# A decoder layer with a mixture of experts: expert results added up in DRAM by accumulating scatters

## The reference, cut to what matters

```
x = x + attention(layernorm(x))            # 16 heads of 64, causal, gated
x = x + retention(layernorm(x), ctx, ctx)  # 16 heads of 8, decay mask
x = x + ffn(layernorm(x))
```

```
topw, sel = top_k(x @ Wg, 3);  topw = softmax(topw)
y_e = gelu(x @ Wup[e] + bup[e]) @ Wdown[e] + bdown[e]     # 128 -> 512 -> 128
ffn(x) = sum over the 3 chosen experts of topw * y_e
```

## Time and profile before

| what | value |
|---|---|
| median of 3 runs | 521.89 us (521.81 to 523.43) |
| profiled execution: time | 523.74 us |
| profiled execution: span of the core | 522.0 us |
| granted TensorE clock, mean | 0.965 |
| PE busy | 457.5 us (88% of the span) |
| DVE busy | 393.2 us (75%) |
| ACT busy | 329.3 us (63%) |
| POOL busy | 256.1 us (49%) |
| DMA read and written in DRAM | 18.91 MB, 11.44 MB |

### The profile page before, as it was taken

The page is one execution under the profiler, slowest core; times in us unless marked ns, Lnnn a source line. Parts: engine busy times, 40 slices in busy tenths (PEclk is TensorE's granted clock), DMA queues, the critical chain, the costliest instruction groups (busy, mean ns, idle before and its releaser), DMA issues.

```text
span 522.0 us, 12401 instructions
## 1 busy us (share of the span) xinstructions
PE 457.5 (88%) x3540; PEld 374.1 (72%) x3540; DVE 393.2 (75%) x1359; ACT 329.3 (63%) x1001; POOL 256.1 (49%) x398
## 2 busy tenths in 40 slices
PE   1689998999999999999999999976697798999980
PEld 1467786877777678687777767854466688999980
DVE  4755477988888888798888888889688766665556
ACT  3558865875776686687577668643445565776660
POOL 3400005157355535726735653575175764666861
PEclk9989999999999999999999999998798898999995
DMA  8990000000000000000000000001045242222248
GB/s 268 367 225 1 1 0 3 1 16 15 10 7 18 15 0 22 13 5 15 15 10 9 19 12 0 22 17 48 20 143 156 68 107 56 74 71 62 63 112 214
DMA packets 40803, 30.06 MB, mean 58 GB/s; under 512 B 3795, under 2 KB 36999, under 8 KB 40768
## 3 DMA queue, kind: packets, MB, share of 16 engines
q1 hardware_dynamic: 36864, 22.63, 15.5%
q0 software_dynamic: 3472, 6.49, 4.0%
q10 hardware_dynamic: 432, 0.53, 0.4%
HBM read 18.91 MB, written 11.44 MB: 58 GB/s over the span
## 4 chain that ended last, share of the span: by engine, by line
PE 52%; DVE 18%; ACT 8%; issue 8%; SPq 5%; POOL 5%; DMA 3%; DVEq 0%; ACTq 0%; POOLq 0%
PE zb L801 8%; PE sc L840 6%; PE ob L869 6%; PE xb L918 4%; PE zb L1074 3%; PE ob L1074 3%; PE xb L943 3%; PE sc L801 2%; PE tb_a L801 2%; ACT pT L667 2%; PE tb_a L853 2%; PE tb_b L853 2%; PE sc L834 2%; DVE nmx L1187 2%; ACT p_sb L660 2%
## 5 line engine op out<-in xcount | busy, mean ns | idle before, releaser
L651 ACT ACTIVATE qk<-zb 128x512 f32<-128x512 f32 x64 | 38.2, 597 | 66.9 <-PE zb L801 66.9
L520 POOL TENSOR_TENSOR spare_p<-tri 128x1 f32<-128x1 f32 x71 | 14.8, 209 | 125.3 <-DVE xn L1268 67.4
L600 POOL DMA_INDIRECT results_by_token<-y_sb,row_i x59 | 60.3, 1022 | 22.3 <-issue 21.8
L658 ACT ACTIVATE p_sb<-sc,nmx 128x128 f32<-128x128 f32 x128 | 47.1, 368 | 33.9 <-DVE nmx L1187 33.5
L660 ACT ACTIVATE p_sb<-sc,nmx 128x256 f32<-128x256 f32 x128 | 61.0, 476 | 0.0
L840 PE MATMUL sc<-qk 64*128 64x256 f32 (+1 forms) x512 | 60.4, 356 | 0.2 <-ACT qk L651 0.2
L869 PE MATMUL ob<-pT,v_sb 128*64 128x256 f32 (+1 forms) x512 | 58.2, 350 | 1.3 <-DVE oT L1205 1.3
L840 PEld LDWEIGHTS sc<-qk 64*128 64x128 f32 x512 | 45.1, 190 | 15.6 <-issue 10.1
L533 POOL DMA_INDIRECT tokens_by_expert<-packed,slot_i x48 | 48.2, 1005 | 8.6 <-issue 7.4
L1205 DVE TENSOR_TENSOR oT<-ob,pT 128x256 f32<-128x256 f32 x64 | 26.9, 420 | 27.1 <-PE ob L869 27.1
L869 PEld LDWEIGHTS ob<-pT,v_sb 128*64 128x64 f32 x512 | 32.3, 141 | 20.8 <-issue 11.2
(11 more groups left out here) (294 smaller groups left out, 1375.4 us busy)
## 6 DMA issues: line engine op xcount, KB each, us to landing
xg<-tokens_by_expert SPq DMA_DIRECT2D x24, 130.0 KB, 2.2
tokens_by_expert<-padding SPq DMA_DIRECT2D x12, 260.0 KB
wup_all<-in_L_ffn_Wup SPq DMA_DIRECT2D x1, 3072.0 KB, 14.4
wdn_all<-in_L_ffn_Wdown SPq DMA_DIRECT2D x12, 256.0 KB, 5.7
wkv_sb<-in_L_attn_Wkv SPq DMA_DIRECT2D x2, 512.0 KB, 6.5
ctx_b<-in_ctx SPq DMA_DIRECT2D x8, 128.0 KB, 2.1
out<-x_all SPq DMA_DIRECT2D x4, 256.0 KB, 3.3
results_by_token<-y_sb,row_i POOLq DMA_INDIRECT x59
```

The lines of the kernel that those rows point to most:

```text
L600: pool.indirect_dma_start(out=ys, out_offset=bass.IndirectOffsetOnAxis(ap=row_i[:, u, a:a + 1], axis=0), in_=y_sb[:, u, a, :], in_offset=None,
L658: act.activation(p_sb[:, w, h, 0:P], sc[:, k, S:S + P], ACT.Exp, bias=nmx[:, w, 0, n:n + 1], accum_out=total[:, w, 0, h:h + 1])
```

## The change

The results are no longer written to rows of their own and added on VectorE, but added up in DRAM. There are two arrays, `sums_of_even_tiles` and `sums_of_odd_tiles`, each with a row for every token and 512 more rows for padding. The scatter of tile n goes to array n % 2 with `compute_op=ALU.add`: the DMA reads the old row, adds, and writes the sum. As two such DMAs on the same rows must not overlap, each waits until the last scatter to its array (tile n-2) has landed. The even array starts as `x2b`: `keep` is now a store by SyncE, and VectorE's next `second_residual` waits for it before it overwrites `x2b`. The odd array is cleared at the start with one DMA from `padding`. Padding rows carry valid row numbers (the 512 rows behind the tokens) in place of `SKIP`, and the bounds check goes. At the end each chunk needs two loads, the even sums straight into `x_all`, and one addition.

```diff
--- before.py
+++ after.py
@@ -39,7 +39,6 @@
 PAD = S + SLOTS
 ROWS = E * CAP + SLOTS
 ROW = D + 2
-SKIP = 1 << 20
 FOUT = 4
 SCALE = DH ** -0.5
 NEG = -3.0e38
@@ -217,7 +216,7 @@
             wv_hi, wv_lo = early("wv_hi", [P, H * DH]), early("wv_lo", [P, H * DH])
             wqk_hi, wqk_lo = early("wqk_hi", [P, 2, H * DH]), early("wqk_lo", [P, 2, H * DH])
         hT = sb("hT", [P, 2, HC, SLOTS])
-        y_in = sb("y_in", [P, TOPK * FOUT * D])
+        sb("rest_of_state", [P, TOPK * FOUT * D])
         y_sb = sb("y_sb", [P, DEPTH, HALVES, D])
         wup_hi = sb("wup_hi", [P, 2, HID], F32R)
         wup_lo = sb("wup_lo", [P, 2, HID], F32R)
@@ -225,9 +224,7 @@
         xgT_lo = sb("xgT_lo", [P, 2, SLOTS], F32R)
         xg = sb("xg", [P, DEPTH, HALVES, ROW])
         sb("rest_of_early", [P, 512])
-        y3 = [a[:, 0:TOPK * FOUT * D].rearrange("p (k n d) -> p k n d", k=TOPK, n=FOUT) for a in (
-            wkv_sb, y_in,
-            p_sb[:, :, :, :].rearrange("p a h k -> p (a h k)"), pT[:, :, :, :].rearrange("p a h k -> p (a h k)"))]
+        odd_sums = wkv_sb[:, :].rearrange("p (n d) -> p n d", n=NT)
         kv_last = wkv_sb[:, :].rearrange("p (t a n) -> p t a n", t=T, a=2)
         spare = sb("spare", [P, 1])
         spare_p = sb("spare_p", [P, 3 + T * TOPK])
@@ -288,7 +285,7 @@
             sem(n) for n in ("ld_x", "ld_xs", "ld_wq", "ld_wk", "ld_wv", "ld_wo", "ld_n", "ld_g", "ld_tab", "ld_bd", "ld_ctx", "ld_up", "ld_dn", "stored"))
         ld_e = [sem(f"ld_e{u}") for u in range(DEPTH)]
         scattered = [sem(f"scattered{u}") for u in range(DEPTH)]
-        dispatched, padded, ld_y = sem("dispatched"), sem("padded"), [sem(f"ld_y{c}") for c in range(NT // FOUT)]
+        dispatched, padded, cleared, kept, ld_y = sem("dispatched"), sem("padded"), sem("cleared"), sem("kept"), [sem(f"ld_y{c}") for c in range(NT // FOUT)]
         consts = sem("consts")
         consts_v = sem("consts_v")
         tables_ready = sem("tables_ready")
@@ -303,8 +300,8 @@
         a_P, a_PA, a_qk, a_hi_wv, a_PT, a_V, a_xT, a_xN, a_ge, a_xn3T, a_el = (
             sem(n) for n in ("a_P", "a_PA", "a_qk", "a_hi_wv", "a_PT", "a_V", "a_xT", "a_xN", "a_ge", "a_xn3T", "a_el"))
         a_kv, v_kv = sem("a_kv"), sem("v_kv")
-        p_kv, p_q, p_sum, p_ret, p_pack, p_keep, p_cell, p_chain = (
-            sem(n) for n in ("p_kv", "p_q", "p_sum", "p_ret", "p_pack", "p_keep", "p_cell", "p_chain"))
+        p_kv, p_q, p_sum, p_ret, p_pack, p_cell, p_chain = (
+            sem(n) for n in ("p_kv", "p_q", "p_sum", "p_ret", "p_pack", "p_cell", "p_chain"))
         pe_CNT, v_hit, v_filled, v_slot, v_pad, v_first, v_plan, v_fin = (sem(n) for n in ("pe_CNT", "v_hit", "v_filled", "v_slot", "v_pad", "v_first", "v_plan", "v_fin"))
         f_row = sem("f_row")
         f_T, f_hi, f_w, f_xg, f_up, f_gelu, f_dn, f_y, f_out = (
@@ -312,7 +309,7 @@
 
 
         xs = nc.dram_tensor("tokens_by_expert", (ROWS, ROW), F32, kind="Internal").ap()
-        ys = nc.dram_tensor("results_by_token", (TOPK * N, D), F32, kind="Internal").ap()
+        ys = [nc.dram_tensor(f"sums_of_{name}_tiles", (N + PAD, D), F32, kind="Internal").ap() for name in ("even", "odd")]
 
         def at(b, per, k):
 
@@ -364,9 +361,22 @@
                 sp.dma_start(wdn_all[:, e, :, :], f_wdown[e].rearrange("(c p) d -> p c d", p=P)).then_inc(ld_dn, 16)
 
             ctx_v = ctx.rearrange("b (t p) d -> b p t d", p=P)
-            with sp.Fori(0, B - 1) as i:
-                sp.wait_ge(p_kv, at((i, 1), T, 0))
-                sp.dma_start(ctx_b[:, :, :], ctx_v[bass.ds(i + 1, 1)].rearrange("a p t d -> p (a t) d")).then_inc(ld_ctx, 16)
+            kept_v = ys[0][0:N, :].rearrange("(b t p) d -> b p t d", t=T, p=P)
+
+            def keep(b):
+
+                sp.wait_ge(v_x2, at(b, 1, 1))
+                to = kept_v[b] if isinstance(b, int) else kept_v[bass.ds(b[0], 1)].rearrange("a p t d -> p (a t) d")
+                sp.dma_start(to, x2b[:, :, :]).then_inc(kept, 16)
+
+            sp.wait_ge(tables_ready, 8)
+            sp.dma_start(ys[1].rearrange("(n p) d -> p n d", p=P), bc(padding[:, 0, 0:D], 1, (N + PAD) // P)).then_inc(cleared, 16)
+            sp.wait_ge(p_kv, T)
+            sp.dma_start(ctx_b[:, :, :], ctx_v[1]).then_inc(ld_ctx, 16)
+            with sp.Fori(0, B - 2) as i:
+                sp.wait_ge(p_kv, at((i, 2), T, 0))
+                sp.dma_start(ctx_b[:, :, :], ctx_v[bass.ds(i + 2, 1)].rearrange("a p t d -> p (a t) d")).then_inc(ld_ctx, 16)
+                keep((i, 0))
 
 
             def load(n):
@@ -390,12 +400,14 @@
             sp.wait_ge(v_first, 1)
             for n in range(DEPTH):
                 load(n)
+            keep(B - 2)
             sp.wait_ge(v_pad, 1)
             with sp.Fori(0, E) as i:
                 r = sp.value_load(pad_row[0:1, bass.ds(i, 1)], min_val=0, max_val=E * CAP - PAD)
                 sp.dma_start(xs[bass.ds(r, PAD), :].rearrange("(a p) w -> p a w", p=P), padding[:, :, :]).then_inc(padded, 16)
             for n in range(DEPTH, EARLY):
                 load(n)
+            keep(B - 1)
             sp.wait_ge(v_plan, 1)
             for n in range(EARLY, TILES):
                 if n == BIG - 1:
@@ -407,11 +419,10 @@
                                      max_val=results_before(TILES + (u - TILES) % DEPTH)) for u in range(DEPTH)]
             for u in range(DEPTH):
                 sp.wait_ge(scattered[u], reached[u])
-            y_v = ys.rearrange("(k n p) d -> p k n d", k=TOPK, p=P)
             for c in range(NT // FOUT):
-                for k in range(TOPK):
-                    n = slice(c * FOUT, (c + 1) * FOUT)
-                    sp.dma_start(y3[c][:, k, :, :], y_v[:, k, n, :]).then_inc(ld_y[c], 16)
+                n = slice(c * FOUT, (c + 1) * FOUT)
+                for sums, to in zip(ys, (x_all, odd_sums)):
+                    sp.dma_start(to[:, n, :], sums[0:N, :].rearrange("(n p) d -> p n d", p=P)[:, n, :]).then_inc(ld_y[c], 16)
             out_v = out.rearrange("b (t p) d -> p (b t) d", p=P)
             for c in range(NT // FOUT):
                 n = slice(c * FOUT, (c + 1) * FOUT)
@@ -448,10 +459,10 @@
             pool.iota(steps256[:, :], [[SLOTS, N // SLOTS]], base=0, channel_multiplier=0, **exact).then_inc(tables_ready, 1)
             pool.iota(steps128[:, :], [[P, N // P]], base=0, channel_multiplier=0, **exact).then_inc(tables_ready, 1)
             pool.iota(tau[:, :], [[1, LATE]], base=0, channel_multiplier=0, **exact).then_inc(tables_ready, 1)
-            pool.iota(result_row[:, :, :], [[P, T], [N, TOPK]], base=0, channel_multiplier=1).then_inc(tables_ready, 1)
+            pool.iota(result_row[:, :, :], [[P, T], [0, TOPK]], base=0, channel_multiplier=1).then_inc(tables_ready, 1)
             pool.memset(padding[:, :, 0:D], 0.0)
             pool.memset(padding[:, :, D + 1:ROW], 0.0).then_inc(tables_ready, 1)
-            pool.iota(padding[:, :, D:D + 1].bitcast(I32), [[0, PAD // P], [0, 1]], base=SKIP, channel_multiplier=0).then_inc(tables_ready, 1)
+            pool.iota(padding[:, :, D:D + 1].bitcast(I32), [[P, PAD // P], [0, 1]], base=N, channel_multiplier=1).then_inc(tables_ready, 1)
 
             pool.affine_select(out=upto[:, :, :], in_=upto[:, :, :], compare_op=ALU.is_ge, fill=0.0, base=0,
                                pattern=[[1, E], [-1, E]], channel_multiplier=0).then_inc(tables_ready, 1)
@@ -546,12 +557,6 @@
                 for n in range(T * TOPK):
                     send(b, n)
 
-            def keep(b):
-
-                pool.wait_ge(v_x2, at(b, 1, 1))
-                carry(2)
-                pool.tensor_copy(x_all[:, bass.ds(tile_of(b, 0), T), :], x2b[:, :, :]).then_inc(p_keep, 1)
-
             def first_half(b, cur):
                 begin(b)
                 send(b, 0)
@@ -571,7 +576,6 @@
                     retained(b, t)
                     if older is not None:
                         send(older, 4 + t)
-                keep(b)
                 pack(b)
                 outer(after(b))
                 first_half(b, after(after(b)))
@@ -588,19 +592,25 @@
             retained(B - 2, 1)
             send(B - 3, 5)
             products(0, kv_last).then_inc(p_kv, 1)
-            keep(B - 2)
             products(1, kv_last).then_inc(p_kv, 1)
             pack(B - 2)
             def scatter(n):
                 u = n % DEPTH
                 pool.wait_ge(p_cell, n + 1)
+                if n == 0:
+                    pool.wait_ge(cleared, 16)
+                    pool.wait_ge(kept, 16 * (B - 2))
+                if n == EARLY:
+                    pool.wait_ge(kept, 16 * B)
+                if n > 1:
+
+                    pool.wait_ge(scattered[(n - 2) % DEPTH], results_before(n - 2 + DEPTH))
                 pool.wait_ge(f_y, n + 1)
                 carry(3).then_inc(p_cell, 1)
                 for a in range(halves(n)):
                     pool.indirect_dma_start(
-                        out=ys, out_offset=bass.IndirectOffsetOnAxis(ap=row_i[:, u, a:a + 1], axis=0),
```

(23 more changed lines are left out.)

## The result

The changed kernel takes 536.14 us in the median of 4 runs (534.8 to 537.57), the kernel before 521.85; the ratio is 1.027, 95% interval 1.0238 to 1.0302. It is slower by 2.7%, where I had forecast 518.7. The profiled execution took 536.39 us around a span of 534.6, 12.6 more than the 522.0 of before.

What follows compares the result with a forecast made beforehand. TensorE was taken to bound the expert stage, bytes moved the end. The sum 491.63 + 12.0 + 15.16 = 518.8, 3.2 us under the 522.0 span, gave a median of 518.7; range 516.0 to 525.0.

Steps and rivals of the forecast that it cites:

- What bounds the kernel now: Whole kernel: TensorE bounds the expert stage with scatters hidden; bytes moved by the full DMA engines bound the end.
- Parts 1 and 2: Kernel's end: final loads 12 to 8, 14.38 to 10.66 us; additions 12 to 4, 1.43 us saved.
- The sum that I wrote for the end: First final load to span end: 10.66 + 1.0 + 0.03 + 0.71 + 2.76 = 15.16 us, against 19.31.
- Part 4: Scatters, tightest in small tiles 23 to 29: each waits for the last but one; final loads start at 503.63, 0.94 late.
- L: Time from an accumulating scatter's issue to its landing, taken as 3.0 us, between bounds of 2.10 and 3.77.
- each microsecond of L costs four: Odd array, tiles 23 to 29: final loads start at 491.63 + 4L, from L = 2.87 on.
- link of 0.40 us: Time GpSimd needs from a DMA's landing to the next scatter's issue, taken as 0.40 us.
- Part 5: Scatter issue on GpSimd: accumulating one takes the present 0.99 us; 0.37 us more per scatter would cost nothing.
- Rival B: Accumulating issue longer on GpSimd: about 536 at 2.0 us an issue, break-even at 1.5; chance 0.09.
- Rival C: Kernel's end: an empty tile's scatter ends it; third lands at 518.8, or near 521; chance 0.08, of which 0.05 still faster.
- Rival A: Odd array, tiles 23 to 29: accumulating landings become the bound from L = 3.80; 524.7 median at 4.5; chance 0.16.
- Parts 3, 6 and 7: Written padding rows at the end, 1.0 us; x2b stores moved to SyncE, nothing; clearing the odd array, hidden, at most 4.7.

Runs made afterwards that it cites:

- The end cut alone: The kernel before with eight final loads and four additions, one result of three left out of the sum: 520.9 us, ratio 0.9988.

## Why the prediction was wrong

**What bounds the kernel now** was read rightly up to a point: scatters hidden behind TensorE, the end bound by bytes. What I did not look at was the closing drain, because it counts as no busy time. It ended 1.4 us ahead of the stores; the 4.15 us that I counted at the end were not to be had with the last scatter where it stood. The end cut alone won 2.0 there.

**Parts 1 and 2 (loads and additions)** had the right size: 13.4 and 13.5 us from the first load to the end, with the drain out of the way, against 15.16 less the 1.0 for empty scatters, so 0.7 less than forecast. The sum that I wrote for the end, 15.16, was 4.8 too small against 19.99, since it left a term out: the last scatter's issue and the drain behind it.

**Part 4 (the wait).** The landing takes 3.4 us in the median (3.2 at least):

```profile
DMA to landing us min/median/max: 3.2/3.4/6.7
```

I had taken 3.0, between my bounds. Of the 1.0 us over the 2.4 of the same kernel's plain scatters, the issue is 0.56; the other 0.4 come after it and are, by this subtraction, what reading and adding add.

The Trainium skill's 0.2 us for an average access to HBM ("DMA: Bandwidth & Descriptors", "Latency and other measured facts") is nearer to this 0.4 than a second round of 2.0 us would be, the reading of "Anatomy of one DMA — SWDGE (gpsimd) path" that gave L = 4.3. Neither section prices the longer issue.

But "each microsecond of L costs four" was not what happened: it assumed a GpSimd that is idle between small tiles. With issues of 1.55 us it takes 1.95 to 1.98 us a small tile without any close wait, 2.05 to 2.18 with it; from tile 9 on the wait adds 0.3 to 0.9 us before the loads in all. My link of 0.40 us was short as well: without a bound and a MOVE, a scatter that has waited still needs 0.45 us after the carry, not 0.15 as a send does, so the link is 0.7 us:

```profile
442.17 0.19 POOL L531 TENSOR_TENSOR spare_p<-tri 128x1 f32<-128x1 f32 x1 [1.00 <-DVE y_sb L1525]
442.81 1.73 POOL L611 DMA_INDIRECT sums_of_odd_tiles<-y_sb,row_i  x1 [0.45 <-issue]
```

**Part 5 (the issue) is the step that failed.** I took 0.99 us for the accumulating issue, for want of a row, and argued from scatters and sends alike that the issue is a fixed sum. It is, nearly, but a different one when it accumulates: 1.55 us. That is 0.56 more per scatter where by my own sum 0.37 were free, so GpSimd and not TensorE sets the pace: 3.88 us a large tile from tile 9 to 23 in place of 3.39, and 11.1 us more up to the first final load. Put into the kernel before by itself, the accumulation costs 10.5 us from tile 9 on; taken out of the kernel after, the pace is back at 3.39.

**Rival B** had the mechanism and its sign, issues over 1.4 us, and its chance of 0.09 was too low. That the issue hardly goes by the row, the runs show too. Its break-even, 1.5 us an issue, was also wrong, on both sides of the sum. The loss: I wrote (2 x 0.52 - 0.74) x 14; measured, tile 9 to 23 took 54.35 us against 47.39, 0.50 a tile and not 0.30 to 0.38, and the small tiles and landings add 3.8. The gain against it: 4.2 was counted, and nothing came. So an issue of 1.55 us, barely over my break-even, comes with a span 12.6 us longer. That the time is near the 536 that B gave for 2.0 us is chance.

**Rival C** was right in kind and came on top, with its sign too (the additions are done 9 us before the end): the empty scatters end the kernel. I let the end wait for the landing of the last one; it waits for the drain, some 5 us more. **Rival A** did not decide: L is 3.4, under the 3.80 from which it would, and the waits' price is small.

**Parts 3, 6 and 7.** The clearing and the stores of x2b delayed nothing to be seen: with all of them in, plain writes kept tile 2 to 23 at 75.4 us. Written padding rows alone were not tried, since two scatters may then write the same row without a wait between. Of the 0.8 us before tile 2 no cause was settled: the five kernels with these stores scatter tile 2 at 412.8 to 415.2, the five without at 412.3 to 414.0, so a price of up to a microsecond there is neither shown nor excluded.

No version beat the kernel before with whole results. With 0.30 us between them, two accumulating issues a large tile take 3.80 us against TensorE's 3.43, and nothing of the other steps changes that.

## What to carry to other kernels

Before an engine that issues DMAs gets a dearer kind of issue, count its time for each tile against the bound engine's: 0.56 us more per issue, twice a tile, was more than the slack of 0.74 us a tile and then set the pace. Before laying a difference of 1 or 2 us to an edit, compare the granted clock of the same stretch in both profiles: here a fall for 3.5 us in one of them was worth up to 1.8 us. Before shortening a kernel's end, list all that must be over before it, the closing drain of GpSimd among them, which no table of busy time shows; here it ended 6 to 9 us after the last scatter's issue, so the last scatter has to be moved forward too or the cut is worth nothing.

## What the runs showed of the hardware

- An accumulating scatter of 128 rows of 512 bytes takes GpSimd 1.55 us to issue against 0.99 for a plain one, and 3.4 against 2.4 us to land, both in the same kernel but for that. With 64 rows it is 1.43 us to issue. While the final loads fill the engines, one of 128 rows takes up to 6.7 us to land.
- GpSimd's DRAIN at the kernel's end is over 8.4 to 9.1 us after the end of its last scatter's issue in seven of the ten kernels profiled, and 6.3 to 6.8 in three, those that accumulate and let each scatter wait for the last but one. What it waits for in that time no run shows; the core's other traffic it is not, as it ended at 508.5 in a kernel that issues its loads from 501.2 to 510.5, each 2.9 us or more from landing.
